# Softmax division with heads on partitions, and a projection of two 128-row products per tile

## The chip, the cores and the metric

One core of one Trainium2 chip runs the kernel. The metric is device time in microseconds from launch to end; lower is better. The engines are TensorE (PE in the rows, its weight loads PEld), VectorE (DVE), ScalarE (ACT), GpSimd (POOL) and SyncE (SP, which issues most transfers). Each runs its own queue in order, and they meet through semaphores.

## What is computed

The input is 16 images of 16x16 positions with 96 channels, that is 4096 tokens. A group norm and a mixture of five 96x96 experts come first, then attention over each image's 256 tokens, then a mixture of four feed-forward experts. The change concerns the attention:

```python
k = jnp.einsum('btc,hcd->bhtd', x, wk)
q = jnp.einsum('btc,hcd->bhtd', x, wq)
v = jnp.einsum('btc,hcd->bhtd', x, wv)
wei = jnp.einsum('bhtd,bhsd->bhts', k, q) / C ** 0.5
wei = jnp.where(causal, wei, -jnp.inf)
wei = jax.nn.softmax(wei, axis=-1)
out = jnp.einsum('bhts,bhsd->bhtd', wei, v)
out = out.transpose(0, 2, 1, 3).reshape(B, T, C)
out = out @ wproj + bproj
```

There are 6 heads of 16 channels. All values are float32.

## The kernel before, in words

The work is cut into 8 units of two images (4 tiles of 128 tokens). Each unit goes through some fifteen kinds of step: `xt` and the group norm, `conv` (first experts), `mix`, `norm1_t`, `qk`, `v`, `score`, `shift`, `prob`, `pv`, `out_t`, `heads_t`, `proj`, `norm2_t`, `gate2`, `ffn1` (12 blocks) and `ffn2` (4 experts). The table `ORDER` lists for each engine, as text, every step in the order in which that engine runs it; `pv.0@3` is part 0 of `pv` of unit 3, and on PE a number behind a colon is the PSUM bank. So the order of work is fixed by hand, on every engine, for all 8 units, and a step that comes late holds up all steps behind it on its engine. `warm` steps (line 800) are matmuls on constants whose results nobody reads; there are 153 of them, nearly all in the first 95 us.

The steps that the change touches, for one unit:

- `pv` (line 931) multiplies the unnormalised probabilities by `v_aug`, which holds 16 channels of V, a column of ones and 15 columns of zeros per head. Its output has heads on partitions: 32 partitions per head (16 channels, the softmax sum in the 17th, zeros), 4 heads side by side, tokens along the row. Twelve head-images make 3 "rounds"; `pv.0` makes two rounds in one bank (128x512), `pv.1` the third (128x256).
- ScalarE copies both banks to `att_t` (line 750).
- `out_t` (line 940): six transposes on PE put tokens on partitions. VectorE then takes the reciprocal of 12 sums per token (line 1182) and multiplies (line 1186) into `att`, once for each of two halves.
- `heads_t` (line 947): four transposes bring `att` back to channels on partitions, in the order of the reference; ScalarE copies it to `heads_t` (line 757), which has a 97th row of ones for the bias.
- `proj` (line 955): one product of 97 rows for each of four tiles. A float32 product is two instructions on PE. VectorE adds the residual (line 1195), takes row statistics, and the second layer norm and the feed-forward part of the unit follow.

On PE the steps of different units are interleaved: while unit n is in attention, PE also runs `ffn1` and `ffn2` of unit n-1 or n-2. One `ffn1` block is three matmuls of 512 columns (lines 787 to 789); one `ffn2` expert is a bias matmul (line 988) and 24 instructions of line 994. VectorE also reduces the scores to row maxima (lines 1152 and 1163), mixes experts (1113 and 1234) and splits values into high and low parts (1131 and 1138).

Of the kernel before, what the change touches and what calls it, by code (L numbers as in the profile page):

```python
# [17 lines left out]
E1 = 4  # L18
# [39 lines left out]
        conv.3@4:6 score.0.0@0:4 score.0.1@0:0 score.0.2@0:3 score.0.3@0:6 score.0.4@0:2 score.1.0@0:5 norm1_t@2:4
        score.1.1@0:0 score.1.2@0:3 score.1.3@0:6 score.1.4@0:4 warm.18@11:2 shift@0:2 qk.0@2:5 qk.1@2:0 warm.2@12:3
        score.0.0@1:3 score.0.1@1:6 score.0.2@1:4 prob.0.0@0:2 score.0.3@1:1 prob.0.1@0:5 score.0.4@1:3 score.1.0@1:6  # L60
        score.1.1@1:4 prob.0.2@0:1 prob.0.3@0:2 prob.0.4@0:3 score.1.2@1:5 prob.1.0@0:1 score.1.3@1:6 prob.1.1@0:4
        score.1.4@1:2 prob.1.2@0:3 prob.1.3@0:5 prob.1.4@0:1 warm.8@13:6 shift@1:6 pv.0@0:4 pv.1@0:2 v@2:3 out_t.0@0:5
        out_t.1@0:1 prob.0.0@1:0 prob.0.1@1:6 prob.0.2@1:4 prob.0.3@1:2 prob.0.4@1:3 heads_t@0:5 prob.1.0@1:0
        prob.1.1@1:1 prob.1.2@1:6 prob.1.3@1:4 proj@0:5 prob.1.4@1:2 warm.3@14:3 score.0.0@2:3 score.0.1@2:0
        score.0.2@2:1 score.0.3@2:6 score.0.4@2:4 score.1.0@2:2 score.1.1@2:5 pv.0@1:3 pv.1@1:0 score.1.2@2:1
        conv.0@5:3 conv.1@5:0 conv.2@5:6 norm2_t@0:4 score.1.3@2:3 score.1.4@2:2 conv.3@5:5 out_t.0@1:0 out_t.1@1:1
        ffn1.0@0:4 ffn1.1@0:3 gate2@0:2 heads_t@1:0 ffn1.2@0:1 ffn1.3@0:6 ffn1.4@0:5 norm1_t@3:0 proj@1:2 shift@2:4
        ffn1.5@0:3 ffn2.0@0:1 ffn2.1@0:6 v@3:4 norm2_t@1:5 ffn1.6@0:2 qk.0@3:3 ffn1.7@0:0 ffn1.8@0:1 ffn1.9@0:4
        ffn1.10@0:2 ffn2.2@0:6 qk.1@3:0 ffn1.11@0:3 prob.0.0@2:1 prob.0.1@2:5 prob.0.2@2:4 prob.0.3@2:2 ffn2.3@0:6
        norm1_t@4:3 prob.0.4@2:0 prob.1.0@2:1 prob.1.1@2:5 prob.1.2@2:4 gate2@1:2 ffn1.0@1:6 prob.1.3@2:0 prob.1.4@2:1  # L70
        conv.0@6:5 conv.1@6:4 conv.2@6:0 conv.3@6:2 ffn1.1@1:1 ffn1.2@1:5 pv.0@2:3 score.0.0@3:4 ffn1.3@1:0 ffn1.4@1:2
        score.0.1@3:6 score.0.2@3:1 ffn1.5@1:3 ffn1.6@1:4 score.0.3@3:5 score.0.4@3:0 pv.1@2:6 score.1.0@3:2
        ffn1.7@1:3 out_t.0@2:1 out_t.1@2:4 score.1.1@3:5 score.1.2@3:6 score.1.3@3:0 score.1.4@3:3 qk.0@4:2 qk.1@4:1
        heads_t@2:4 ffn1.8@1:5 ffn1.9@1:6 ffn1.10@1:4 ffn1.11@1:0 ffn2.0@1:5 proj@2:6 shift@3:3 v@4:4 ffn2.1@1:0
        ffn2.2@1:2 prob.0.0@3:1 conv.0@7:5 norm2_t@2:3 ffn2.3@1:4 prob.0.1@3:6 prob.0.2@3:0 prob.0.3@3:1 prob.0.4@3:5
        norm1_t@5:2 prob.1.0@3:3 prob.1.1@3:6 prob.1.2@3:0 conv.1@7:4 gate2@2:1 prob.1.3@3:5 prob.1.4@3:3
        score.0.0@4:6 ffn1.0@2:0 ffn1.1@2:5 ffn1.2@2:3 ffn1.3@2:1 qk.0@5:4 qk.1@5:2 ffn1.4@2:6 pv.0@3:0 score.0.1@4:5
        score.0.2@4:4 ffn1.5@2:3 score.0.3@4:2 score.0.4@4:1 score.1.0@4:5 conv.2@7:6 conv.3@7:0 score.1.1@4:4
        score.1.2@4:3 score.1.3@4:2 score.1.4@4:6 pv.1@3:1 v@5:0 out_t.0@3:5 out_t.1@3:1 ffn2.0@2:4 shift@4:3
        ffn1.6@2:0 ffn1.7@2:2 ffn1.8@2:6 ffn1.9@2:5 score.0.0@5:1 ffn1.10@2:3 ffn1.11@2:0 heads_t@3:2 score.0.1@5:6  # L80
        prob.0.0@4:4 score.0.2@5:5 prob.0.1@4:3 prob.0.2@4:1 proj@3:0 prob.0.3@4:2 ffn2.1@2:6 ffn2.2@2:5 prob.0.4@4:4
        score.0.3@5:3 score.0.4@5:1 prob.1.0@4:2 prob.1.1@4:0 prob.1.2@4:6 norm2_t@3:4 prob.1.3@4:5 prob.1.4@4:2
        ffn2.3@2:0 gate2@3:6 norm1_t@6:4 score.1.0@5:3 pv.0@4:5 pv.1@4:2 score.1.1@5:1 ffn1.0@3:0 out_t.0@4:6
        out_t.1@4:5 ffn1.1@3:4 qk.0@6:2 score.1.2@5:6 score.1.3@5:5 qk.1@6:0 heads_t@4:4 score.1.4@5:3 v@6:2
        ffn1.2@3:4 ffn1.3@3:0 proj@4:1 ffn2.0@3:2 ffn1.4@3:4 ffn1.5@3:0 ffn1.6@3:6 ffn1.7@3:1 ffn1.8@3:5 ffn2.1@3:4
        shift@5:2 norm2_t@4:0 ffn1.9@3:3 ffn1.10@3:6 ffn1.11@3:1 ffn2.2@3:5 score.0.0@6:2 prob.0.0@5:4 prob.0.1@5:3
        norm1_t@7:0 prob.0.2@5:6 prob.0.3@5:1 ffn2.3@3:5 score.0.1@6:2 prob.0.4@5:4 prob.1.0@5:3 prob.1.1@5:6
# [1177 lines left out]
```

## Time and profile before

| | us |
|---|---|
| median of 3 runs | 353.42 |
| lowest and highest | 352.49, 353.59 |
| the profiled execution's own time | 352.74 |
| its span, first to last instruction | 351.0 |

Busy, in the span: PE 335.9 us, PE's weight loads 273.5, DVE 231.2, ACT 231.8, POOL 107.8. The mean granted clock of TensorE was 0.988 of full speed. Between 100 and 300 us PE was busy for 199.76 of 200 us and VectorE for 139.41. The last chain of work lies for 77% of the span on PE. A mean duration in a group of rows is that of one instruction from start to end; since matmuls overlap, PE's pace is read from the starts of instructions that follow one another or from the chain of waits, not from the mean.

### The profile page before, as it was taken

The page shows a single profiled execution, that of the slowest core. Times are in us where ns is not written, and L with a number is a line of the kernel's source. Part 1 is how long each engine was busy: PE and PEld are TensorE (multiplying, and loading weights), DVE is VectorE, ACT ScalarE, POOL GpSimd, SP SyncE. Part 2 cuts the span into 40 slices and gives each one's busy share as a digit, 9 for nine tenths or more (in the row PEclk, how much of TensorE's full clock was granted, in tenths as well). Part 3 has the DMA queues.
Part 4 walks back from the last instruction along what each step waited for, and adds up shares of the span by engine and source line. Part 5 has one row for each costly group of instructions (what it writes and reads, how often), then busy time and mean ns, then how long its engine had stood idle before and what let it go on. Part 6 is the DMA issues. An engine that isn't in the chain of part 4 may idle for free.

```text
span 351.0 us, 7705 instructions
## 1 busy us (share of the span) xinstructions
PE 335.9 (96%) x2627; PEld 273.5 (78%) x2627; DVE 231.2 (66%) x1025; ACT 231.8 (66%) x467; POOL 107.8 (31%) x179
## 2 busy tenths in 40 slices
PE   6889998879999999999999999999999999999995
PEld 3655466546788987789878988898799789889895
DVE  4859895977379789868686698747647623453232
ACT  3777873555779689548864866497916977374460
POOL 3457761535432224043340434303410305001000
...
GB/s 189 168 4 0 2 35 102 76 63 57 82 3 1 4 67 92 2 52 89 22 69 69 4 23 25 114 5 22 80 57 4 25 2 2 24 1 2 22 2 23
DMA packets 24123, 14.80 MB, mean 42 GB/s; under 512 B 14323, under 2 KB 24083, under 8 KB 24084
## 3 DMA queue, kind: packets, MB, share of 16 engines
...
## 4 chain that ended last, share of the span: by engine, by line
PE 77%; DVE 6%; ACT 6%; DMA 4%; POOL 2%; ACTq 2%; issue 2%; SPq 1%; DVEq 0%; POOLq 0%
PE PS L994 24%; PE PS L787 10%; PE PS L789 9%; PE PS L788 9%; DMA k_stack<-qk_parts 4%; PE PS L931 4%; PE PS L889 3%; PE PS L913 3%; PE PS L840 2%; PE PS L955 2%; PE PS L800 2%; ACTq L684 2%; PE PS L988 2%; PE PS L878 1%; PE PS L940 1%
## 5 line engine op out<-in xcount | busy, mean ns | idle before, releaser
L994 PEld LDWEIGHTS PS<-w_f,hidden 128*128 128x128 f32 x768 | 90.0, 192 | 0.1
L994 PE MATMUL PS<-w_f,hidden 128*128 128x96 f32 x768 | 90.0, 274 | 0.0
L780 ACT ACTIVATE hidden<-PS 128x512 f32<-128x512 f32 x96 | 54.9, 596 | 29.5 <-PE PS L789 27.5
L1234 DVE SCALAR_TENSOR_TENSOR res<-PS,weight,res 128x96 f32<-128x96 f32 x128 | 31.7, 311 | 48.3 <-PE PS L994 48.2
L1152 DVE CUSTOM_DVE_ANT_0 masked<-PS,causal 128x128 bf16<-128x128 f32 (+1 forms) x120 | 35.1, 353 | 9.5 <-PE PS L878 7.4
L787 PE MATMUL PS<-t_hi,w_hi 97*128 97x512 f32 x96 | 40.9, 426 | 0.0
L800 PE MATMUL PS<-ones_b 128*128 128x512 bf16 x153 | 37.0, 391 | 3.4 <-POOL ones_b L518 3.4
L789 PE MATMUL PS<-t_hi,w_lo 97*128 97x512 f32 x96 | 38.1, 397 | 0.0
L788 PE MATMUL PS<-t_lo,w_hi 96*128 96x512 f32 x96 | 38.1, 397 | 0.0
L622 POOL TENSOR_SCALAR_AFFINE_SELECT prob_a<-prob_a 128x768 f32<-128x768 f32 x16 | 13.9, 866 | 65.5 <-ACT prob_a L742 65.5
L1113 DVE SCALAR_TENSOR_TENSOR PS<-conv_y,weight,PS 128x96 f32<-128x96 f32 x128 | 30.3, 315 | 5.1 <-ACT PS L694 5.0
L800 PEld LDWEIGHTS PS<-ones_b 128*128 128x128 bf16 x153 | 14.7, 101 | 20.1 <-issue 5.5
L742 ACT ACTIVATE prob_a<-PS 128x512 f32<-128x512 f32 x48 | 26.1, 610 | 5.9 <-PE PS L913 5.9
L634 ACT ACTIVATE normed<-res,ln_bias,ln_scale 128x96 f32<-128x96 f32 x64 | 24.5, 457 | 2.8 <-POOL ln_bias L543 2.8
L613 POOL TENSOR_SCALAR qk_parts<-qk_rest 96x512 bf16<-96x512 f32 x16 | 9.9, 617 | 49.2 <-DVE qk_rest L1138 32.2
L789 PEld LDWEIGHTS PS<-t_hi,w_lo 97*128 97x128 f32 x96 | 18.2, 190 | 4.3
L533 POOL TENSOR_TENSOR ln_var<-ln_mv,eps_t 128x4 f32<-128x4 f32 x16 | 3.2, 198 | 59.5 <-DVE ln_mv L1045 59.5
L787 PEld LDWEIGHTS PS<-t_hi,w_hi 97*128 97x128 f32 x96 | 18.2, 190 | 3.5 <-issue 0.4
L788 PEld LDWEIGHTS PS<-t_lo,w_hi 96*128 96x128 f32 x96 | 18.2, 189 | 2.7
L679 ACT ACTIVATE conv_y<-PS 128x486 f32<-128x486 f32 x32 | 17.4, 567 | 2.9 <-PE PS L789 2.1
L616 POOL TENSOR_TENSOR qk_parts<-qk_rest,qk_parts 96x512 bf16<-96x512 f32 x16 | 18.5, 1157 | 2.4
L1163 DVE TENSOR_REDUCE row_max<-PS 128x2 f32<-128x512 f32 (+2 forms) x30 | 17.3, 626 | 0.6 <-PE PS L889 0.4
...
## 6 DMA issues: line engine op xcount, KB each, us to landing
...
```

Of the source, the lines that this page charges most:

```text
L616: pool.tensor_tensor(qk_parts[:, tensor, 2, cols], qk_rest[:, tensor, cols], qk_parts[:, tensor, 1, cols], ALU.subtract).then_inc(low_read ...
L634: act.activation(normed[:, which, t, :], rows[:, t, :], ACT.Identity, bias=ln_bias[:, which, t:t + 1], scale=ln_scale[:, which, t:t + 1]). ...
L742: act.activation(dst, PS[:, bank("prob", n, index), 0:dst.shape[1]], ACT.Exp, scale=SCALE).then_inc(act_emptied["prob"], 1)
L780: act.activation(hidden[:, m, 0:T * P], PS[:, bank("ffn1", n, index), 0:T * P], ACT.Gelu).then_inc(act_emptied["ffn1"], 1)
L787: pe.matmul(dst, a_hi, b_hi, start=True, stop=False)
L788: pe.matmul(dst, a_hi[0:b_lo.shape[0], :], b_lo, start=False, stop=False)
L789: return pe.matmul(dst, a_lo, b_hi[0:a_lo.shape[0], :], start=False, stop=True)
L800: pe.matmul(PS[:, bank("warm", n, index), :], ones_b[:, :], ones_b[:, :].unsqueeze(1).to_broadcast([P, 4, P]), start=True, stop=True)
L994: mm = pe.matmul(PS[:, y, t * C:(t + 1) * C], hidden[:, m, t * P:(t + 1) * P], w2_f[:, m, :], start=False, stop=t == T - 1 and c == CHUNKS ...
L1113: ins = dve.scalar_tensor_tensor(mixed[:, t, :], y, weight0[:, t, e:e + 1], mixed[:, t, :], ALU.mult, ALU.add)
L1152: ins = dve.tensor_tensor_reduce(masked[:, place % 2, j * size:(j + 1) * size], ps[:, j * size:(j + 1) * size], causal[:, TOKENS - size:TO ...
L1234: ins = dve.scalar_tensor_tensor(res2[:, t, :], PS[:, y, t * C:(t + 1) * C], weight1[:, t, e:e + 1], res2[:, t, :], ALU.mult, ALU.add).the ...
```

## The change

`out_t` and `heads_t` are gone from every engine, and so are the tiles `inv_sum`, `att` and `heads_t` and ScalarE's two copies of the `pv` banks. In their place VectorE has a step `att` in two parts, for the 512 and the 256 columns that `pv` made. Each part is three instructions on all 128 partitions: `stream_shuffle` reads the `pv` bank and writes, to every partition of a group of 32, the row of that group's 17th partition (the sums); `reciprocal` inverts this whole tile in place; a multiply of the `pv` bank by it writes `att_t`. So `att_t` now holds normalised heads on partitions, with a 1 in each 17th row.

The projection's weight `wproj_r` is stored to match: 128 rows with 16 used of every 32, and 3 slices; row 16 of the first slice holds the bias, all other rows are zero. `proj` is now two accumulated products of 128 rows per tile: one of the image's own four heads, one of the round that holds heads 4 and 5 of both images. `pv` deals the heads to the rounds in that manner. The weight comes in 4 transfers and the bias in one, so that `FFN_LOADS` is 13 instead of 10; the row of ones of `heads_t` needs no transfer any more (`LATE_PADS` 4 instead of 5), and one memset of `wproj_r` (`PADS` 6 instead of 5) is new on VectorE. The tables of all five engines are written anew; there are 154 warm matmuls instead of 153.

```diff
+        wproj_r = sb("wproj_r", [P, 3, C])
-        inv_sum = sb("inv_sum", [P, 2, 2 * HEADS])
-        att = sb("att", [P, TILES, C])
-        heads_t = sb("heads_t", [C + 1, PT])
+        sums = sb("sums", [P, 2 * TOKENS])
...
-        CONV_PADS, PADS, LATE_PADS = 5, 5, 5
-        FFN_LOADS = 10
+        CONV_PADS, PADS, LATE_PADS = 5, 6, 4
+        FFN_LOADS = 13
...
+            wproj_heads = wproj.rearrange("(h d) c -> d h c", d=D)
+            for j in range(HG):
+
+                other = 1 + j // 2
+                ffn_loads.append((wproj_r[HS * j:HS * j + D, 0:other + 1:other, :],
+                                  wproj_heads[:, j:HG + j % 2 + 1:HG + j % 2 - j, :]))
+            ffn_loads.append((wproj_r[D:D + 1, 0, :], bproj.rearrange("(a n) -> a n", a=1)))
...
-                elif kind == "pv":
-                    b = index[0]
-                    wait_filled(act, "pv", n, index)
-                    if n > 0:
-                        wait_filled(act, "out_t", n - 1, (1,))
-                    rounds = (slice(0, 2), slice(2, ROUNDS))[b]
-                    act.activation(att_t[:, rounds, :].rearrange("p r t -> p (r t)"),
...
-                elif kind == "heads_t":
-                    wait_filled(act, "heads_t", n)
...
-                                image, h = divmod(HG * r + j, HEADS)
+                                image, h = ((0, j), (j // 2, HG + j % 2), (1, j))[r]
...
-                elif kind == "out_t":
-                    t = index[0]
-                    wait_bank_free(pe, "out_t", n, index)
-                    wait_act(pe, "pv", n, (1,))
-                    for r in range(ROUNDS):
-                        mm = pe.transpose(PS[:, bank("out_t", n, index), r * P:(r + 1) * P],
-                                          att_t[:, r, t * P:(t + 1) * P], ident[:, :])
-                    mm.then_inc(filled["out_t"], 1)
-                elif kind == "heads_t":
-                    wait_bank_free(pe, "heads_t", n)
-                    wait_dve(pe, "out_t", n, (W - 1,))
-                    for t in range(T):
-                        mm = pe.transpose(PS[0:C, bank("heads_t", n), t * P:(t + 1) * P], att[:, t, :], ident[:, :])
...
-                    wait_act(pe, "heads_t", n)
-                    for t in range(T):
-                        mm = pe.matmul(PS[:, bank("proj", n), t * C:(t + 1) * C], heads_t[:, t * P:(t + 1) * P],
-                                       wproj_f[:, :], start=True, stop=True)
+                    wait_dve(pe, "pv", n, (1,))
+                    for image in range(W):
+                        for half in range(2):
+                            t, rows = 2 * image + half, slice(half * P, (half + 1) * P)
+                            pe.matmul(PS[:, bank("proj", n), t * C:(t + 1) * C], att_t[:, 2 * image, rows], wproj_r[:, 0, :],
+                                      start=True, stop=False)
+                            mm = pe.matmul(PS[:, bank("proj", n), t * C:(t + 1) * C], att_t[:, 1, rows],
+                                           wproj_r[:, 1 + image, :], start=False, stop=True)
...
+            dve.memset(wproj_r[:, :, :], 0.0).then_inc(pad_ready, 1)
...
-                elif kind == "out_t":
...
-                    step_done(dve.reciprocal(inv_sum[:, t, :], rows[:, :, D]))
...
+                elif kind == "att":
+
+                    r = index[0]
+                    rounds = (slice(0, 2), slice(2, ROUNDS))[r]
+                    width = (rounds.stop - rounds.start) * TOKENS
+                    heads = PS[:, bank("pv", n, index), 0:width]
+                    wait_filled(dve, "pv", n, index)
+                    if nth("pv", n, index) > 1:
+                        dve.wait_ge(dve_emptied["pv"], nth("pv", n, index) - 1)
+                    step_done(dve.stream_shuffle(sums[:, 0:width], heads, [D] * HS))
                     wait_step()
+                    step_done(dve.reciprocal(sums[:, 0:width], sums[:, 0:width]))
+                    wait_step()
+                    if n > 0:
+                        wait_filled(dve, "proj", n - 1)
+                    dve.tensor_tensor(att_t[:, rounds, :].rearrange("p r t -> p (r t)"), heads, sums[:, 0:width],
+                                      ALU.mult).then_inc(dve_emptied["pv"], 1)
```

How the instructions stand on the engines is shown at two places. The first is PE in the last unit, unit 7. Before, between the end of `pv` and `proj` stand the last three transposes of `att_t` (line 940), three `ffn1` blocks, the transposes of `att` (line 947), one `ffn2` expert, and then `proj` (line 955):

```order
L940 MATMUL PS<-ident,att_t 128x128 x3
...
L788 MATMUL PS<-t_lo,w_hi 128x512
L789 MATMUL PS<-t_hi,w_lo 128x512
L947 MATMUL PS<-ident,att 96x128 x4
L988 MATMUL PS<-b_parts,ones_b 128x384
L994 MATMUL PS<-w_f,hidden 128x96 x12
L955 MATMUL PS<-wproj_f,heads_t 128x96 x4
```

Now, in the same unit (`pv` is line 918, `ffn1` lines 774 to 776, `ffn2` lines 965 and 971, `proj` lines 930 and 932):

```order
L918 MATMUL PS<-prob_a,v_aug 32x256 x4
L918 MATMUL PS<-prob_b,v_aug 32x128 x4
L774 MATMUL PS<-t_hi,w_hi 128x512
L775 MATMUL PS<-t_lo,w_hi 128x512
L776 MATMUL PS<-t_hi,w_lo 128x512
...
L965 MATMUL PS<-b_parts,ones_b 128x384
L971 MATMUL PS<-w_f,hidden 128x96 x12
L930 MATMUL PS<-wproj_r,att_t 128x96
L932 MATMUL PS<-wproj_r,att_t 128x96
```

No transpose stands there any more; between the last `pv` matmul and the first of `proj` lie two `ffn1` blocks and one `ffn2` expert, and one more `ffn1` block lies between `pv.0` and `pv.1`.

The second place is VectorE in unit 1. Before, the two `out_t` halves stand behind the row maxima of unit 2's scores (line 1163), and the shift of unit 2 follows:

```order
L1163 TENSOR_REDUCE row_max<-PS 128x2 x2
L1182 RECIPROCAL inv_sum<-PS 128x12
L1186 TENSOR_TENSOR att<-PS,inv_sum 128x2x96
L1182 RECIPROCAL inv_sum<-PS 128x12
L1186 TENSOR_TENSOR att<-PS,inv_sum 128x2x96
L1169 TENSOR_SCALAR shift_parts<-row_max 128x4x6
```

Now (row maxima are line 1141):

```order
L1109 TENSOR_TENSOR t2_lo0<-PS,t2_hi0 96x512
L1165 STREAM_SHUFFLE sums<-PS 128x512
L1167 RECIPROCAL sums<-sums 128x512
L1171 TENSOR_TENSOR att_t<-PS,sums 128x512
L1141 TENSOR_REDUCE row_max<-PS 128x2
L1165 STREAM_SHUFFLE sums<-PS 128x256
L1167 RECIPROCAL sums<-sums 128x256
L1171 TENSOR_TENSOR att_t<-PS,sums 128x256
L1141 TENSOR_REDUCE row_max<-PS 128x2
L1147 TENSOR_SCALAR shift_parts<-row_max 128x4x6
```

Two row maxima now stand behind the first and the second part of `att`, and both reciprocals are over all columns.

## Rows read from the trace of the kernel before

**Rows 1.** The page: busy time by engine, and chain that ended last, by engine.
```profile
PE 335.9 (96%) x2627; PEld 273.5 (78%) x2627; DVE 231.2 (66%) x1025; ACT 231.8 (66%) x467; POOL 107.8 (31%) x179
...
PE 77%; DVE 6%; ACT 6%; DMA 4%; POOL 2%; ACTq 2%; issue 2%; SPq 1%; DVEq 0%; POOLq 0%
```

**Rows 2.** Windows of core 0: start:end, length, busy per engine, PEclk, DMA share.
```profile
106.30:146.60 40.30, 40.30 (x320) 34.08 (x320) 34.05 (x158) 33.00 (x68) 11.33 (x17) 1.00 0.14 36
147.20:185.60 38.40, 38.22 (x321) 32.74 (x320) 29.19 (x147) 25.97 (x52) 13.58 (x20) 1.00 0.24 59
...
100.00:300.00 200.00, 199.76 (x1703) 172.82 (x1701) 139.41 (x681) 145.06 (x286) 55.17 (x87) 1.00 0.16 37
```

**Rows 3.** The chain of waits in order of time: start us, us, what.
```profile
143.96 0.45 PE PS L889 x4
...
211.04 0.66 PE PS L940 x6
...
252.47 0.44 PE PS L947 x4
...
259.25 0.89 PE PS L955 x8
```

**Rows 4.** Timeline of PE, units 6 and 7: start us, us, line, out<-in, count.
```profile
297.88 0.64 PE L931 MATMUL PS<-prob_a,v_aug 128*32 128x256 f32 x8
...
299.20 0.61 PE L931 MATMUL PS<-prob_a,v_aug 128*32 128x256 f32 x8
...
308.34 0.39 PE L787 MATMUL PS<-t_hi,w_hi 97*128 97x512 f32 x1
...
309.03 0.39 PE L787 MATMUL PS<-t_hi,w_hi 97*128 97x512 f32 x1
...
310.17 0.33 PE L988 MATMUL PS<-b_parts,ones_b 128*128 128x384 bf16 x1
...
313.18 1.10 PE L955 MATMUL PS<-wproj_f,heads_t 97*128 97x96 f32 x8
```

**Rows 5.** Groups on VectorE by form: count, busy us, mean ns, idle before.
```profile
L1163 DVE TENSOR_REDUCE row_max<-PS 128x2 f32<-128x512 f32 x18 | 11.7, 679 | 0.4 <-PE PS L889 0.4
...
L1138 DVE TENSOR_TENSOR qk_rest<-PS,qk_parts 96x512 f32<-96x512 f32 x16 | 10.5, 680 | 6.5 <-ACT qk_parts L716 6.5
...
L1163 DVE TENSOR_REDUCE row_max<-PS 128x2 f32<-128x256 f32 x6 | 2.5, 412 | 0.0
```

**Rows 6.** The same view: reciprocals, and other small instructions beside them.
```profile
L1182 DVE RECIPROCAL inv_sum<-PS 128x12 f32<-128x12 f32 x16 | 3.6, 226 | 10.4 <-PE PS L940 10.3
...
L1221 DVE RECIPROCAL gpinv<-gpeps 128x4 f32<-128x4 f32 x8 | 1.4, 178 | 0.3
...
L1219 DVE SCALAR_TENSOR_TENSOR gpeps<-gsum,gpsum 128x4 f32<-128x4 f32 x8 | 1.4, 174 | 0.3
L1202 DVE COPY gcross<-PS 128x16 f32<-128x16 f32 x8 | 1.4, 173 | 6.8 <-PE PS L968 6.7
```

**Rows 7.** Timeline of VectorE, the `out_t` pair of unit 3 and its neighbour.
```profile
185.40 0.23 DVE L1182 RECIPROCAL inv_sum<-PS 128x12 f32<-128x12 f32 x1
...
186.47 0.25 DVE L1027 TENSOR_TENSOR beats<-conv_y 128x100 f32<-128x100 f32 x1
```

**Rows 8.** Groups on ScalarE by form: the copies of `pv` and `heads_t`.
```profile
L750 ACT ACTIVATE att_t<-PS 128x512 f32<-128x512 f32 x8 | 4.8, 598 | 6.3 <-PE PS L931 6.3
L757 ACT ACTIVATE heads_t<-PS 96x512 f32<-96x512 f32 x8 | 4.7, 591 | 1.3 <-PE PS L947 1.3
...
L750 ACT ACTIVATE att_t<-PS 128x256 f32<-128x256 f32 x8 | 3.1, 384 | 2.0 <-PE PS L931 1.6
```

**Rows 9.** Timeline of SP's queue in the first 20 us.
```profile
11.96 1.22 SPq L468 DMA_DIRECT2D hidden<-in_L_ffn_b_dram  x3
```

**Rows 10.** Timeline of VectorE: its first instruction after the memsets.
```profile
7.22 0.75 DVE L1052 BATCH_NORM_STATS2 gn_stats<-XT 96x6 f32<-96x256 f32 x2 [3.54 <-ACT XT L641]
```

**Rows 11.** Timeline of ScalarE: its first step that waits for the feed-forward loads.
```profile
21.22 0.19 ACT L655 ACTIVATE gate_both<-gate_f 97x4 fp32r<-97x4 f32 x1
```

More of the change, by code:

```diff
@@ L58 @@
[L58 to L87, printed above, removed]
@@ L98 @@
[L98 to L102 removed]
+        gavg.0@1:2 warm.6@3:4 gavg.1@1 warm.2@4:4 conv.0@0:4 conv.1@0:3 conv.2@0:5 conv.3@0:6 gavg.0@2:0 warm.4@5:1
@@ new lines @@
+        prob.0.0@3:1 ffn2.2@1:5 prob.0.1@3:0 prob.0.2@3:4 prob.0.3@3:3 ffn2.3@1:2 norm2_t@2:6 prob.0.4@3:1
+        prob.1.0@3:5 prob.1.1@3:0 conv.0@7:4 conv.1@7:3 conv.2@7:1 prob.1.2@3:6 prob.1.3@3:5 prob.1.4@3:4
+        score.1.0@4:2 conv.3@7:3 gate2@2:1 ffn1.0@2:0 ffn1.1@2:6 score.1.1@4:2 ffn1.2@2:3 score.1.2@4:5 norm1_t@5:4
+        pv.0@3:1 pv.1@3:2 ffn1.3@2:0 ffn1.4@2:5 ffn1.5@2:6 ffn1.6@2:3 ffn1.7@2:4 ffn1.8@2:0 score.1.3@4:5
+        score.1.4@4:6 ffn1.9@2:3 proj@3:1 qk.0@5:4 shift@4:2 ffn1.10@2:0 ffn1.11@2:5 ffn2.0@2:3 qk.1@5:6 ffn2.1@2:2
@@ new lines @@
+        score.1.2@2 mix.1@4 norm2_t@0 att.0@1 score.1.3@2 att.1@1 score.1.4@2 shift@2 gate2@0 proj@1 norm1_t@3 mix.2@4
+        gates.0@5 weights@0 qk.0@3 mix.3@4 mix.4@4 ffn2.0@0 qk.1@3 xadd@4 gates.1@5 ffn2.1@0 stats1@4 mix.1@5
+        norm2_t@1 ffn2.2@0 mix.2@5 mix.3@5 gate2@1 score.0.0@3 norm1_t@4 score.0.1@3 score.0.2@3 gates.0@6 qk.0@4
+        qk.1@4 att.0@2 score.0.3@3 score.0.4@3 score.1.0@3 ffn2.3@0 score.1.1@3 att.1@2 mix.4@5 weights@1 gates.1@6
+        score.1.2@3 score.1.3@3 score.1.4@3 shift@3 ffn2.0@1 ffn2.1@1 score.0.0@4 score.0.1@4 proj@2 score.0.2@4
@@ new lines @@
+        score.0.3@4 xadd@5 score.0.4@4 stats1@5 ffn2.2@1 mix.1@6 mix.2@6 norm2_t@2 ffn2.3@1 mix.3@6 score.1.0@4
+        mix.4@6 gate2@2 score.1.1@4 score.1.2@4 weights@2 norm1_t@5 att.0@3 att.1@3 score.1.3@4 score.1.4@4 shift@4
+        proj@3 gates.0@7 xadd@6 qk.0@5 ffn2.0@2 stats1@6 qk.1@5 ffn2.1@2 gates.1@7 ffn2.2@2 mix.1@7 mix.2@7 mix.3@7
+        mix.4@7 norm2_t@3 ffn2.3@2 norm1_t@6 gate2@3 qk.0@6 score.0.0@5 score.0.1@5 weights@3 qk.1@6 score.0.2@5
+        score.0.3@5 att.0@4 score.0.4@5 score.1.0@5 score.1.1@5 ffn2.0@3 att.1@4 ffn2.1@3 score.1.2@5 score.1.3@5
```

206 lines of the change are left out of this document (99 added, 107 removed).

## The prediction

> **What bounds the kernel now.** I read the page first [rows 1]: PE is busy for 96% of the span, VectorE and ScalarE for 66% each, and the chain that ended last lies for 77% on PE. A share over the whole span hides stages, so the windows come next [rows 2]: from 100 to 300 us PE is busy for 199.76 of 200 us at full clock. So every PE instruction taken out after 100 us is worth its pace, and every microsecond that PE is made to wait there is lost whole, since nothing behind it can be caught up by a full engine. In the same 200 us VectorE has 60.6 us without work, but not evenly: in the two stretches that lie between the `out_t` steps of units 1, 2 and 3 it is busy for 34.05 of 40.3 and 29.19 of 38.4 us.
>
> **What PE saves.** The pace comes from the chain [rows 3]: six transposes of `att_t` take 0.66 us, four of `att` 0.44, eight instructions of `proj` 0.89, so each is 0.11 us whatever it is. Per unit 10 transposes go (1.10 us) and `proj` grows from 8 to 16 instructions (4 tiles, 2 products, 2 instructions each; +0.89 us). The net is 0.21 us, in 8 units **-1.7 us**. The move from 97 to 128 rows and the new head order in `pv` change no count. The 153 warm matmuls become 154, at 0.22 us nothing.
>
> **What ScalarE saves.** 24 copies, 12.6 us of busy time [rows 8]. ScalarE is not what PE waits for (66% busy, PE idle 0.24 us in 200), so I take nothing for it; it only gives its other steps more room.
>
> **What VectorE pays.** Removed per unit are two pairs of reciprocal and multiply; four instructions take 1.07 us from start to the neighbour's start [rows 7]. Added are two triples. The shuffle and the multiply read a PSUM bank: two instructions of quite different kinds over 512 columns take 0.68 us, one over 256 takes 0.41 [rows 5]; I take these for both. No shuffle is in the trace, so its cost is bounded only by these rows, from 0.6 to, if it ran at half their rate, 1.2 us.
>
> The reciprocal is the term that decides. The trace has it only small [rows 6]: 12 elements take 226 ns, 4 elements 178 ns, while other instructions of 4 or 16 elements take 174 and 173. The line through the two is 6.0 ns per element and 154 ns to start: 53 ns above the plain copy for 12 elements, and 4 for 4. Part of the 53 could belong to the reading from PSUM with a stride, in which case a reciprocal would cost like any instruction. So the bounds for 512 columns are 0.65 us (like the rows of 512 columns, from SBUF slightly less) and 154 + 512 x 6.0 = 3.23 us. The two ends differ five-fold. I take the upper, because the copy from PSUM of 16 elements shows that PSUM alone costs nothing extra at this size, and stays 53 ns below with more elements. For 256 columns it is 1.69 us.
>
> The Trainium skill, "VectorE: DVE Perf Modes", in its walkthrough of the 8-slice pipeline, says that the reciprocal is an iterated hardware divide with a repeat count of 8. Read as 8 cycles of its 0.96 GHz per element, that would be an estimate of 8.3 ns per element and 4.4 us for 512 columns; the rows lie lower, at 6.0 ns. It speaks against this change, since the work goes from 12 sums per token to a copy of each sum on every partition and column.
>
> So one `att.0` is 0.68 + 3.23 + 0.68 and two gaps of 0.06 and one to start, 4.8 us; `att.1` is 0.41 + 1.69 + 0.41 and the same gaps, 2.65 us; a unit's chain is **7.5 us** from the end of `pv.0` to the start of `proj`, where before it was copies, transposes and the pairs. Over 8 units VectorE's busy time rises by about 8 x 6.2 = 50 us, to some 280.
>
> **Where PE waits for it.** For each unit I sum what the new order puts on PE between the end of `pv.0` and `proj`, and what it puts on VectorE. The prices [rows 4]: `pv.1` 0.65 us (`pv.0` 1.3, from start to start), an `ffn1` block 0.69, an `ffn2` expert with its bias matmul 3.0 (310.17 to 313.18); transposes and score matmuls are 0.11 each [rows 3].
> - Units 6 and 7: `pv.1`, three `ffn1` and one `ffn2`: 5.7 us against 7.5, so 1.8 us of wait each.
> - Unit 5: `pv.1`, three `ffn1`, four transposes and four score matmuls, 3.6 us: 3.9 us of wait.
> - Unit 4: `att.0` starts late behind two score steps, and three more and an `ffn2` step stand between its parts; 12.3 us on VectorE against 11.9 on PE: 0.4.
> - Unit 3: six `ffn1`, two scores, one `ffn1` and `pv.1`, 6.0 us: 1.5.
> - Unit 2: over 18 us of PE work: none.
> - Unit 1: `pv.1`, two scores, `gate2` and four `ffn1`, 4.9 us; VectorE has a row maximum of 0.68 between the parts, 8.1: 3.2.
> - Unit 0: `pv.1`, `shift`, `v` and five warm matmuls, 3.4 us, so up to 4.1; but PE is not full there, and the new order has the `qk` splits of unit 2 earlier on VectorE, before the scores of unit 1. I take 1.0.
>
> That is 13.6 us. These are waits of a full PE, in order, one behind the other, so they add.
>
> **What else stands behind it on VectorE.** Behind each `att` part are row maxima, `mix`, `ffn2` sums; PE needs their banks. Between units 1, 2 and 3 VectorE had 6.3 and 9.2 us free in the stretches [rows 2], and part of that is gaps between dependent small instructions which no other step can use. The added 6.4 us (7.5 less 1.07) just fills them. I take 4 us of further waits in units 1 to 4, from a lower bound of 0 to 12 (if each of four units loses half of 6.2).
>
> **The start.** The memset of `wproj_r`, even at the 0.68 us of a 512-column instruction, falls into VectorE's idle 3.54 us [rows 10]. Three more transfers cost SP about 0.4 us each (three of line 468 took 1.22) [rows 9]; the last load is issued at 13.2 us now and by 15 then, and its first reader on ScalarE starts at 21.22 us [rows 11]. Nothing, as long as that cover of some 6 us holds; if it were gone, 1 to 2 us. The order of the first 80 us is also new; its chains are the same, and I give it 0 with 1.5 us to either side.
>
> **The sum** against the profiled execution: 352.74 - 1.7 + 13.6 + 4.0 = 368.6 us. The profiled execution was 0.7 below the median of the runs, so for a median that is **369 us**.
>
> **Rivals.**
> *The reciprocal is as cheap as other instructions.* Then `att.0` is 2.1 us and `att.1` 1.4 with gaps, a chain of 3.5 us, and that fits under the PE work of every unit above (3.4 to 18). VectorE rises by some 19 us and still has room. What is left is PE's 1.7 us: 351 profiled, **351.7** as a median, faster by 0.5%. The point from which it decides is a reciprocal below about 1.5 us for 512 columns. For it speaks that a line through two small sizes is extrapolated forty-fold; against it, that the excess appears in both. 0.12.
> *VectorE becomes the bound.* In the stretch from 100 to 200 us its load and the additions meet PE's length. If half of the added 50 us shows on PE instead of 18, then 352.7 - 1.7 + 25 = 376, and with the steps behind it queued in order up to 384. This is also where a reciprocal of 8.3 ns would lead: by the page's figure, 1.8 us more for a unit's chain, 7 units, so 12.6 on top of 369, that is 382. For it speaks VectorE's 84% in the first stretch; against it, 65% and less after 200 us. **376 to 384**, 0.20.
> *The waits hide each other.* Direct waits fall where PE would have waited for ScalarE's `gelu` or the masks anyway, or the stack transfers come earlier because VectorE's `qk` steps do. Before, PE waited 0.24 us in 200, so there is little to hide in; the new order may have made some. **355 to 361**, 0.10.
> My forecast, 361 to 376, has 0.58.
>
> **How the numbers follow.** A measurement of this kernel can tell about 0.3% (1.1 us) from no change. Faster by more than that is most of the first rival, 0.09; within it 0.03, the rest of that case; slower 0.88. The range from 357 to 384 holds the forecast, the second rival nearly whole and a part of the third; the cheap reciprocal and the tail above are left out. The time of the likeliest case is 369.
>
> **What would show it.** In the profile of the changed kernel the rows of line 1167 must show about 3.2 us for 512 columns and 1.7 for 256; at 0.65 the first rival holds, at 4.4 the page's reading. PE's `proj` row (line 930) should name VectorE's `att_t` (line 1171) as what ended its idle time, with some 14 us in about 7 waits and the longest in units 0, 1 and 5; PE's busy share from 100 to 300 us should fall to about 92%. VectorE's busy time should be near 280 us, ScalarE's near 219. If line 1167 is dear but PE is as full as before, the order covers it and my sums of the PE work are wrong.

## The result, and the profile after

| | before | after |
|---|---|---|
| median of 4 runs, us | 352.96 | 390.28 |
| lowest and highest | 351.76, 353.59 | 389.35, 391.1 |
| profiled span | 351.0 | 388.3 |
| PE busy; PE idle in the span | 335.9; 15.1 | 355.5; 32.8 |
| VectorE busy, ScalarE busy | 231.2, 231.8 | 278.2, 216.2 |
| mean granted clock of TensorE | 0.988 | 0.928 |

The changed kernel takes 1.106 times as long (95% interval 1.104 to 1.109): 37.3 us more, where 16 were forecast, and above the range's end of 384. The sign was right, the size was not. The kernel before has one run more here than in the table ahead of the prediction, which moves its median from 353.42 to 352.96.

The page of the changed kernel, engine by engine, the granted clock in 40 slices (tenths of full speed), the chain by engine, and the groups of the two lines that the prediction named; it answers to [rows 1]:

```profile
PE 355.5 (92%) x2612; PEld 286.0 (74%) x2612; DVE 278.2 (72%) x1058; ACT 216.2 (56%) x441; POOL 107.9 (28%) x179
...
PEclk9999999786987999999968969999699998996999
...
PE 69%; DVE 20%; ACT 4%; issue 3%; POOL 2%; DMA 1%; ACTq 1%; DVEq 0%; POOLq 0%
...
L1167 DVE RECIPROCAL sums<-sums 128x512 f32<-128x512 f32 (+1 forms) x16 | 40.8, 2553 | 0.6
...
L930 PE MATMUL PS<-wproj_r,att_t 128*128 128x96 f32 x64 | 17.5, 367 | 15.9 <-DVE att_t L1171 15.9
```

The clock row of the page of before, which no row ahead of the prediction showed:

```profile
PEclk9999999889999999999999999999999999999999
```

Read the first row against [rows 1] before anything else. The span grew by 37.3 us, and PE's two halves share that: 17.7 us more without work, and 19.6 us more **busy**, though PE has 1.7 us less to do. A busy time that grows with less work means slower instructions. The clock row says why: after the first 80 us it never showed less than a 9 before, and now nine slices have an 8, 7 or 6. The groups of VectorE by form (count, busy us, mean ns, idle before) give the new steps' prices:

```profile
L1167 DVE RECIPROCAL sums<-sums 128x512 f32<-128x512 f32 x8 | 26.8, 3353 | 0.3
L1167 DVE RECIPROCAL sums<-sums 128x256 f32<-128x256 f32 x8 | 14.0, 1753 | 0.3
L1165 DVE STREAM_SHUFFLE sums<-PS 128x512 f32<-128x512 f32 x8 | 5.9, 732 | 0.0
L1171 DVE TENSOR_TENSOR att_t<-PS,sums 128x512 f32<-128x512 f32 x8 | 5.5, 692 | 0.3
```

PE's waits (engine, line, what it waited for: us in all, times, longest):

```profile
PE PS L930 <- DVE att_t L1171: 15.9, 7, 4.5
PE PS L774 <- DVE att_t L1171: 3.8, 3, 1.9
```

Ten waits, 19.7 us: `proj` waits for `att_t`, and so does an `ffn1` block (line 774) at three places where its PSUM bank is the one that `pv` held. The longest is in unit 0, where the timeline of PE (start us, us, line, in brackets the idle time before) shows it, and what comes behind:

```profile
87.01 1.25 PE L787 MATMUL PS<-ones_b 128*128 128x512 bf16 x5
92.74 0.71 PE L930 MATMUL PS<-wproj_r,att_t 128*128 128x96 f32 x2 [4.47 <-DVE att_t L1171]
93.24 0.63 PE L932 MATMUL PS<-wproj_r,att_t 128*128 128x96 f32 x2
93.67 0.64 PE L930 MATMUL PS<-wproj_r,att_t 128*128 128x96 f32 x2
94.09 0.63 PE L932 MATMUL PS<-wproj_r,att_t 128*128 128x96 f32 x2
```

A pair of `proj` instructions now starts every 0.43 us, 0.213 for each instruction, where [rows 3] had 0.11. The windows of the changed kernel (start:end, length, busy of PE, PEld, DVE, ACT, POOL, granted clock, DMA share, GB/s) show the clock there, in the stretch of 100 to 300 us of [rows 2], and behind the waits of units 0, 3 and 5:

```profile
100.00:300.00 200.00, 188.30 (x1475) 159.20 (x1474) 157.25 (x630) 116.83 (x240) 52.38 (x84) 0.92 0.17 36
92.70:96.20 3.50, 3.46 (x16) 3.50 (x17) 0.00 (x0) 0.00 (x0) 0.00 (x0) 0.50 0.02 5
...
197.00:203.80 6.80, 6.78 (x26) 5.55 (x27) 4.83 (x27) 1.11 (x2) 1.34 (x3) 0.50 0.00 1
...
275.00:281.90 6.90, 6.90 (x28) 5.73 (x29) 4.62 (x24) 1.19 (x2) 1.48 (x5) 0.53 0.01 2
281.90:286.00 4.10, 4.10 (x39) 3.90 (x39) 1.60 (x5) 1.44 (x4) 3.52 (x5) 1.00 0.00 0
```

A granted clock of 0.50 is 1.2 GHz in place of 2.4. Read the windows in pairs: from 275.0 to 281.9 PE is busy without a gap and gets 28 instructions done; in the 4.1 us that follow it does 39. The two windows hold different instructions (the first has six of 512 columns), so `proj` gives the fair comparison: a pair every 0.43 us here, and every 0.22 us in unit 4, where the clock stayed at 1.00. The busy share is 100% in both windows, which is why the share of PE's busy time alone tells nothing of this loss.

The mean clock gives the total. Time at half clock is twice the span times what the mean lacks of 1: 2 x 388.3 x 0.072 = 55.9 us after, 2 x 351.0 x 0.012 = 8.4 us before. The most that this can cost is half of the difference, **23.8 us**. PE's busy time shows 19.6 + 1.7 = **21.3 us** of it. The rest is half clock in which PE had nothing to run anyway, inside its waits and behind its last instruction: within the stretches of half clock PE is busy for 49.6 us after and 6.8 before, and half of that difference is 21.4. So the 37.3 us of span are 17.7 of idle time, 21.3 of slow clock, and 1.7 saved.

### The profile page after: what moved, and what is told of

It reads as the page before. It is cut to its first block, busy times and chain, and to the rows that moved or that the text cites. A ratio compares the mean times of both kernels' runs of the same rounds, so it can differ in the third digit from the quotient of the medians.

```text
span 388.3 us, 7660 instructions
## 1 busy us (share of the span) xinstructions
PE 355.5 (92%) x2612; PEld 286.0 (74%) x2612; DVE 278.2 (72%) x1058; ACT 216.2 (56%) x441; POOL 107.9 (28%) x179
## 4 chain that ended last, share of the span: by engine, by line
PE 69%; DVE 20%; ACT 4%; issue 3%; POOL 2%; DMA 1%; ACTq 1%; DVEq 0%; POOLq 0%
PE PS L971 19%; DVE sums L1167 10%; PE PS L774 8%; PE PS L775 7%; PE PS L776 7%; PE PS L787 6%; PE PS L930 3%; PE PS L900 3%; PE PS L932 3%; DVE sums L1165 2%; DVE att_t L1171 2%; PE PS L918 2%; PE PS L827 2%; PE PS L876 1%; PE PS L904 1%
## 5 line engine op out<-in xcount | busy, mean ns | idle before, releaser
L971 PEld LDWEIGHTS PS<-w_f,hidden 128*128 128x128 f32 x768 | 93.0, 197 | 0.0
L971 PE MATMUL PS<-w_f,hidden 128*128 128x96 f32 x768 | 92.4, 278 | 0.0
L774 PE MATMUL PS<-t_hi,w_hi 97*128 97x512 f32 x96 | 43.2, 450 | 3.8 <-DVE att_t L1171 3.8
L1167 DVE RECIPROCAL sums<-sums 128x512 f32<-128x512 f32 (+1 forms) x16 | 40.8, 2553 | 0.6
L775 PE MATMUL PS<-t_lo,w_hi 96*128 96x512 f32 x96 | 39.7, 413 | 0.0
L776 PE MATMUL PS<-t_hi,w_lo 97*128 97x512 f32 x96 | 39.5, 412 | 0.0
L744 ACT ACTIVATE prob_a<-PS 128x512 f32<-128x512 f32 x48 | 26.1, 602 | 15.1 <-PE PS L900 15.0
L930 PE MATMUL PS<-wproj_r,att_t 128*128 128x96 f32 x64 | 17.5, 367 | 15.9 <-DVE att_t L1171 15.9
L787 PEld LDWEIGHTS PS<-ones_b 128*128 128x128 bf16 x154 | 14.7, 101 | 19.6 <-issue 5.8
L930 PEld LDWEIGHTS PS<-wproj_r,att_t 128*128 128x128 f32 x64 | 13.9, 268 | 18.4 <-issue 13.2
L774 PEld LDWEIGHTS PS<-t_hi,w_hi 97*128 97x128 f32 x96 | 19.5, 203 | 9.7 <-DVE att_t L1171 5.1
L718 ACT ACTIVATE qk_parts<-PS 96x512 bf16<-96x512 f32 x16 | 8.9, 592 | 21.8 <-PE PS L776 17.6
```

The source lines that it names most:

```text
L744: act.activation(dst, PS[:, bank("prob", n, index), 0:dst.shape[1]], ACT.Exp, scale=SCALE).then_inc(act_emptied["prob"], 1)
L774: pe.matmul(dst, a_hi, b_hi, start=True, stop=False)
L775: pe.matmul(dst, a_hi[0:b_lo.shape[0], :], b_lo, start=False, stop=False)
L776: return pe.matmul(dst, a_lo, b_hi[0:a_lo.shape[0], :], start=False, stop=True)
L787: pe.matmul(PS[:, bank("warm", n, index), :], ones_b[:, :], ones_b[:, :].unsqueeze(1).to_broadcast([P, 4, P]), start=True, stop=True)
L930: pe.matmul(PS[:, bank("proj", n), t * C:(t + 1) * C], att_t[:, 2 * image, rows], wproj_r[:, 0, :], start=True, stop=False)
```

## Experiments

All are one core and one launch; each ratio is to the kernel before on the same chip. The kernel before took 351.87 us beside e1 to e4, 352.55 beside e5 to e8 and 352.96 beside the changed kernel, so a difference between the medians of two different kernels is good to about 1 us. Two theories stood at the outset. **A**: the long reciprocal makes PE wait some 20 us, and each wait is followed by a stretch of half clock that costs about as much again. **B**: the waits alone are not the cause; VectorE's work as a whole, or the new PE part (`pv` and `proj` in 128 rows), makes the kernel longer.

### Fill the waits with work nobody reads (e1_fill)

84 more warm matmuls stand in front of the instructions that waited, about as long as the waits; nothing else is changed. Two of the nine places:

```diff
-        pv.1@0:4 shift@1:3 v@2:6 warm.5@17:5 proj@0:5 prob.0.0@1:1
+        pv.1@0:4 shift@1:3 v@2:6 warm.25@17:5 proj@0:5 prob.0.0@1:1
...
-        score.1.4@4:6 ffn1.9@2:3 proj@3:1 qk.0@5:4
+        score.1.4@4:6 ffn1.9@2:3 warm.12@20:4 proj@3:1 qk.0@5:4
```

> The changed kernel, with warm matmuls (0.22 us each) added on PE in front of the places where its trace shows PE waiting for att_t: 20 more in unit 0, 6 and 7 in unit 1, 12 in unit 3, 5 in unit 4, 8 and 8 in unit 5, 10 in unit 6, 8 in unit 7. Nothing that is used is computed otherwise. In the trace of the changed kernel PE is without work for 32.8 us (15.1 before) and the granted clock is 0.5 in some 58 us (10 before). Theory A, the waits and the half clock that follows each of them: the waits stay (18 us), the half clock goes, time 370 to 374 us, mean clock above 0.97. Theory B, VectorE's load is the bound and PE's clock only shows that PE has less to do: time stays at 388 to 392 us, the warm matmuls change nothing. Theory C, the clock costs half of what its share suggests: 380.

Measured: 374.3 us (373.65 to 377.45), ratio 1.065 (1.061 to 1.070). The kernel does 18.6 us more on PE than the changed one and is 16.0 us shorter (15 if each is set against the kernel before on its own chip). Its page, its waits for `att_t`, and one new wait:

```profile
PE 358.2 (95%) x2696; PEld 279.4 (74%) x2696; DVE 277.3 (74%) x1058; ACT 215.9 (57%) x441; POOL 107.6 (29%) x179
...
PEclk9999999989978999999999969999999999999999
```

```profile
PE PS L787 <- ACT hidden L767: 2.9, 2, 2.2
...
PE PS L774 <- DVE att_t L1171: 0.5, 1, 0.5
...
PE PS L930 <- DVE att_t L1171: 0.2, 1, 0.2
```

VectorE does the same work in the same order, so what went is not its load. In the profiled execution PE's idle time fell from 32.8 to 17.5 us and the matmuls added 18.6, so by themselves they made the kernel 3.3 us longer; the span is 12.6 us shorter all the same, so the clock gave back 15.9. The time at half clock fell from 55.9 to 2 x 375.7 x 0.023 = 17.3 us, worth up to 19.3. Theory A holds: a little over half of the loss sits in the clock. The profiled run of this kernel was its longest (clock 0.977, against 0.988 to 0.994 in the others), so by medians the clock gives back 18 to 19; the size is good to about 3 us.

Three stretches of half clock are left in this trace before the end. One lies behind a wait for a stack transfer, as in the changed kernel. One begins within the wait of 2.2 us in the first row above, in which the added matmuls themselves wait for a bank. The third, from 218.1 to 224.9 us, has no wait ahead of it; it comes back under "What stays open".

### Leave the reciprocal out (e2_cheap)

```diff
-                    step_done(dve.reciprocal(sums[:, 0:width], sums[:, 0:width]))
+                    step_done(dve.tensor_copy(sums[:, 0:width], sums[:, 0:width]))
```

The division is left out; every wait, tile and table stays.

> The changed kernel with the reciprocal of the sums replaced by a copy of the same tile in place, so the division is left out; all waits and all other instructions stay. A copy of 512 columns should take 0.3 to 0.7 us instead of 3.35, VectorE's busy time falls by 33 us or more. Theory A and B alike say that the reciprocal's length is the whole cause: 351 to 353 us, clock near 0.985, PE's 1.7 us saving just visible. If something else in the new order, the two products or the 13 loads costs time, the result is above 355.

Measured: 350.38 us (349.25 to 351.91), ratio 0.9955 (0.9938 to 0.9972). The group of line 1167, and the page's engines:

```profile
PE 332.4 (96%) x2612; PEld 269.2 (77%) x2612; DVE 244.9 (70%) x1058; ACT 215.7 (62%) x441; POOL 107.8 (31%) x179
```

```profile
L1167 DVE COPY sums<-sums 128x512 f32<-128x512 f32 x8 | 4.1, 507 | 0.3
```

One line sets the whole loss. A unit's two reciprocals are (3.35 - 0.51) + (1.75 - 0.29) = 4.3 us longer than the copies, 34.4 us of VectorE in 8 units, and the kernel is 39.9 us longer for it. It is also the prediction's first rival, played out: with a cheap step in this place the change is 0.45% **faster** than before, 1.5 us, which is about PE's 1.7 us. Theory B's second half falls: the new PE part is as good as was reckoned.

### Take the reciprocal off the chain, but keep its work (e3_off_chain)

The copy stands in the chain as above, and the two reciprocals run behind the multiply into a tile that nobody reads. The division is left out here too.

```diff
-                    step_done(dve.reciprocal(sums[:, 0:width], sums[:, 0:width]))
+                    step_done(dve.tensor_copy(sums[:, 0:width], sums[:, 0:width]))
...
+                    step_done(dve.reciprocal(spare[:, 0:width], sums[:, 0:width]))
+                    wait_step()
```

> As the kernel with the copy in the reciprocal's place (the division is left out), but the same reciprocals (512 and 256 columns per unit) are made behind the multiply of each part, into a tile that nobody reads. VectorE's load is that of the changed kernel plus the copies, about 285 us; only the first part's multiply and its bank come 3 us earlier, while the second part still stands behind the first reciprocal. Theory A, the chain from pv to proj is what PE waits for: the chain falls from 7.5 to about 6 us, the third of it that lay in the second reciprocal is gone, so the waits fall from 18 to 5 to 9 us and the clock loss with them: 360 to 372. Theory B, the load: 386 to 392.

Measured: 383.38 us (381.07 to 384.81), ratio 1.089 (1.085 to 1.093). This is outside what either theory gave, and against me: I had thought that off the chain most of the price would go. PE's waits, and three rows of VectorE's timeline at the place where unit 2's first part is done:

```profile
PE PS L931 <- DVE att_t L1172: 9.6, 7, 3.3
...
PE PS L886 <- DVE shift_parts L1155: 2.5, 3, 1.3
...
PE PS L775 <- DVE row_max L1142: 1.8, 1, 1.8
PE PS L775 <- DVE row_max L1131: 1.6, 1, 1.6
```

```profile
149.36 0.69 DVE L1172 TENSOR_TENSOR att_t<-PS,sums 128x512 f32<-128x512 f32 x1
149.97 3.34 DVE L1174 RECIPROCAL spare<-sums 128x512 f32<-128x512 f32 x1
153.34 0.43 DVE L1131 CUSTOM_DVE_ANT_0 masked<-PS,causal 128x256 bf16<-128x256 f32 x1
```

The masks and row maxima of the next unit stand directly behind the reciprocal in VectorE's queue and start when it ends. Half of the waits for `att_t` are gone, since only the first part's reciprocal still stands ahead of the second part; in their place come waits for `shift_parts` and `row_max`. Their sum, with the 9.6, is 15.5 us. So it is not the dependence alone that costs but the 3.35 us in an in-order queue, wherever PE is this full: theory A's "chain of `att`" was too narrow, and half of B is right, in that whoever is queued behind pays.

### The same reciprocals in the kernel before (e4_before_recip)

The kernel before, with a reciprocal of 512 and one of 256 columns of a spare tile ahead of each unit's two `out_t` parts.

```diff
+                    width = 2 * TOKENS if t == 0 else TOKENS
+                    step_done(dve.reciprocal(spare[:, 0:width], spare[:, 0:width]))
+                    wait_step()
```

> The kernel before with one idle reciprocal of 512 columns ahead of the first out_t half and one of 256 ahead of the second on VectorE, in a tile that nobody reads: the old transposes and the old projection with VectorE's new cost (5.1 us per unit). Summing as in the prediction what its order puts on PE between the transposes and heads_t (1 to 2.6 us in units 0, 1, 2, 4, 5, 8 in unit 3), PE waits some 20 us. Theory A: 352.7 + 20 + about 20 for the half clock, 385 to 400 us, so the changed kernel's new PE part is innocent. Theory B, load: VectorE at 272 of 352 us still has room, 355 to 365. If the new PE part or the new order were at fault: 353 to 358.

Measured: 403.17 us (402.09 to 404.69), ratio 1.146 (1.143 to 1.150), somewhat above what was expected. PE's waits for `att`:

```profile
PE PS L948 <- DVE att L1191: 19.9, 6, 5.2
PE PS L890 <- DVE att L1191: 4.3, 2, 2.4
...
PE PS L788 <- DVE att L1191: 3.1, 2, 2.4
```

The old kernel, whose table was not written for such a step, suffers more: 27.3 us of waits, PE's busy time 356.7 in place of 335.9. This leaves the new tables of the changed kernel as no cause; they soften the blow, if anything.

### Order on PE alone (e6_order)

In units 3 and 6, steps that need nothing from `att` are moved ahead of `proj`; VectorE's list is untouched.

```diff
-        score.1.4@4:6 ffn1.9@2:3 proj@3:1 qk.0@5:4 shift@4:2 ffn1.10@2:0 ffn1.11@2:5 ffn2.0@2:3
+        score.1.4@4:6 ffn1.9@2:3 qk.0@5:4 ffn1.10@2:0 ffn2.0@2:3 proj@3:1 shift@4:2 ffn1.11@2:5
...
-        ffn2.0@5:6 proj@6:0 shift@7:4
-        ffn2.1@5:3 ffn2.2@5:5
+        ffn2.0@5:6 ffn2.1@5:3 proj@6:0 shift@7:4
+        ffn2.2@5:5
```

> The changed kernel with PE's table changed in two units only: in unit 3 qk.0 of unit 5, ffn1.10 and ffn2.0 of unit 2 stand before proj instead of behind it (4.4 us of work against a wait of 2.7), in unit 6 ffn2.1 of unit 5 (2.8 us against 2.2). VectorE's work and order are untouched. Theory A: the two waits (4.9 us) and the half clock behind them (3.4 us each, 5 where the stretch at 0.5 is 10 us long) go: 377 to 382 us against 390. Theory B (VectorE's load): 388 to 392, since VectorE does the same in the same order.

Measured: 381.43 us (381.22 to 383.12), ratio 1.084 (1.081 to 1.086).

```profile
PE 349.3 (92%) x2612; PEld 281.3 (74%) x2612; DVE 276.9 (73%) x1058; ACT 215.9 (57%) x441; POOL 107.5 (28%) x179
```

```profile
PE PS L930 <- DVE att_t L1171: 9.8, 5, 4.5
```

Seven waits of `proj` became five, 6.1 us less in sum, but PE's idle time fell by 2.7 us only, since new waits came (the longest, 1.3 us, for a stack transfer). The span is 8.9 us shorter: 2.7 less idle time, and 6.2 less **busy** time for the same 2612 instructions. Again the clock pays more than the waits themselves.

### One wait, and one wait filled (e7_one_wait, e8_one_filled)

To see the price of a single stretch, the kernel before gets the two spare reciprocals in unit 5 only (e7); in e8, in addition, 18 warm matmuls stand ahead of `heads_t@5`.

```diff
+                    width = 2 * TOKENS if t == 0 else TOKENS
+                    if n == 5:
+                        step_done(dve.reciprocal(spare[:, 0:width], spare[:, 0:width]))
+                        wait_step()
```

```diff
-        heads_t@5:6 ffn1.9@4:4 ffn2.0@4:5
+        warm.18@18:6 heads_t@5:6 ffn1.9@4:4 ffn2.0@4:5
```

> The kernel before with idle reciprocals of 512 and 256 columns on VectorE in unit 5 alone, ahead of the two out_t halves. In the run that had them in all units PE waited 4.1 us there before heads_t. Theory A: one wait of 4.1 us and one stretch of half clock of 6.8 us, worth 3.4 us where PE is full: 351.9 + 7.5, so 358.5 to 360. Theory B: VectorE is half idle in that stretch, so the wait alone at most: 352 to 356.

> As the kernel with reciprocals in unit 5 alone, and 18 warm matmuls (3.9 us) on PE before heads_t of unit 5, in the place of the wait. Theory A: the wait stays as warm work, the half clock goes: 351.9 + 4.1, so 355.5 to 356.5, 3 us or more below the same kernel without them. If the clock has no part in it: the same time as without them.

Measured: e7 358.06 us (357.73 to 359.3), ratio 1.018 (1.015 to 1.020); e8 356.46 (355.17 to 357.97), ratio 1.012 (1.009 to 1.014). e7 lies just below what was expected of it and e8 at the upper end. The timeline of PE in e7 behind the wait, and the same window of 15 us in before, e7 and e8, in this order:

```profile
255.75 1.06 PE L948 MATMUL PS<-ident,att 128*96 128x128 f32 x4 [4.08 <-DVE att L1192]
```

```profile
250.00:265.00 15.00, 15.00 (x124) 13.87 (x122) 8.28 (x50) 6.73 (x14) 1.52 (x4) 1.00 0.35 75
```

```profile
250.00:265.00 15.00, 10.92 (x74) 9.64 (x73) 8.69 (x24) 3.04 (x6) 0.00 (x0) 0.89 0.32 64
```

```profile
250.00:265.00 15.00, 14.91 (x101) 11.44 (x100) 10.25 (x31) 4.85 (x8) 0.93 (x1) 1.00 0.36 80
```

One wait of 4.1 us, and a clock of 0.89 in the window: (1 - 0.89) x 15 x 2 = 3.3 us at half clock, worth 1.7. In e8 the wait's time is still spent, on matmuls that nobody reads, but the clock stays at 1.00, and the kernel is 1.6 us shorter. I had expected 3 us or more, since I took a stretch of 6.8 us as in the changed kernel; here it was 3.3. The mechanism held, the size was half. The 1.6 us rests on the medians of five and six runs, whose mean granted clocks are 0.988 and 0.995 on average (worth up to 2.5 us). The two profiled executions show it only in this window: e7's was its shortest run and e8's its longest, their spans are 356.0 and 356.2 us, and e7 has one stretch of half clock fewer in its first 80 us. What a wait costs beyond itself was thus 1.6 us in this place. Over the changed kernel there were 21.3 us of slow clock beside 19.7 us of waits, though up to 3.4 of the 21.3 lie in a stretch that has no wait ahead of it.

### The division with 16 and 8 elements (e5_turned)

If only the number of elements is at fault, the division should be free with fewer. This kernel computes the whole result: it transposes the `pv` bank in blocks of 32x32, so that the sums of a block's 32 tokens stand in one column, takes the reciprocal of 16 (or 8) such columns, and transposes that column, repeated 32 times, back into the tile of factors.

```diff
-                    step_done(dve.stream_shuffle(sums[:, 0:width], heads, [D] * HS))
+                    blocks = width // HS
+                    step_done(dve.transpose(turned[:, 0:width], heads))
...
-                    step_done(dve.reciprocal(sums[:, 0:width], sums[:, 0:width]))
+                    step_done(dve.reciprocal(inverse[:, 0:blocks],
+                                             turned[:, 0:width].rearrange("p (b d) -> p b d", d=HS)[:, :, D]))
+                    wait_step()
+                    step_done(dve.transpose(sums[:, 0:width].rearrange("p (b d) -> p b d", d=HS),
+                                            inverse[:, 0:blocks].unsqueeze(2).to_broadcast([P, blocks, HS])))
```

> The changed kernel, complete, with the same division made on few elements: VectorE transposes the pv bank in blocks of 32x32, so that the sums of a block stand in one column; the reciprocal is over 16 (8) elements instead of 512 (256); a second block transpose of the inverted column, read 32 times, spreads it over the 32 partitions; then the multiply. Orders are untouched. From the trace of the changed kernel: 0.73 + 0.25 + 0.7 + 0.69 and gaps, 2.6 us for the first part and 1.7 for the second, a chain of 4.3 us against 7.5 there and 3.4 in the kernel with the copy, 0 to 1 us of PE wait in unit 0 and none elsewhere. Theory A: 350 to 354 us, clock above 0.98. If a transpose of blocks runs at half rate or does not take a repeated input at full rate, 355 to 365. Theory B (load): VectorE is at about 255 us, 350 to 354 too; this run is for the version, not for telling A from B.

Measured: 352.32 us (351.78 to 355.01) against 352.55, ratio 1.002 (0.9995 to 1.0046): no difference from before that can be measured, and 38 us shorter than the changed kernel. Five of its twelve runs took 354.7 to 355.0 us at a mean granted clock of 0.979, the other seven 351.8 to 352.6 us at 0.988 to 0.995; no trace shows where the half clock of those five lies. Its groups on VectorE, and PE's wait for it:

```profile
L1173 DVE STREAM_TRANSPOSE sums<-inverse 128x512 f32<-128x512 f32 x8 | 5.7, 711 | 0.3
L1168 DVE STREAM_TRANSPOSE turned<-PS 128x512 f32<-128x512 f32 x8 | 5.7, 710 | 4.4 <-PE PS L920 4.4
...
L1170 DVE RECIPROCAL inverse<-turned 128x16 f32<-128x16 f32 x8 | 2.0, 253 | 0.3
L1170 DVE RECIPROCAL inverse<-turned 128x8 f32<-128x8 f32 x8 | 1.6, 204 | 0.3
```

```profile
PE PS L932 <- DVE att_t L1178: 1.6, 2, 1.0
```

Four instructions take 0.71 + 0.25 + 0.71 + 0.69 = 2.4 us where the changed kernel's three take 4.8. PE's busy time is 333.6, close to e2's 332.4. The span is 2.3 us above e2's, the best that this layout has shown; I found no version that clearly beats the kernel before.

## Why the prediction missed

**PE's own work** (-1.7 us): right. It shows wherever the clock does not hide it: e2 is 1.5 us shorter than the kernel before.

**The prices on VectorE**: right. The reciprocal was forecast at 3.23 and 1.69 us and took 3.35 and 1.75; of the two ends of that bound, five-fold apart, the upper was the true one, and the small excess of [rows 6] was the sign of it. The shuffle took 0.73 against 0.68. A unit's chain ran from 84.92 to 92.6 in unit 0, 7.7 us against 7.5. VectorE's busy time is 278.2 against 280, ScalarE's 216.2 against 219.

The Trainium skill, "VectorE: DVE Perf Modes", in its walkthrough of the 8-slice pipeline, gives the repeat count of 8 that I had read as 8.3 ns per element. It does not fit as I read it: between 256 and 512 columns the trace gives (3353 - 1753) / 256 = 6.25 ns. The measurement decides, and the second rival's 382, which rested on 8.3, has no ground.

**The waits**: right in sum, by luck in part. PE's idle time rose by 17.7 us against 13.6 + 4.0 = 17.6, but the first term was 6 us too small and the second 6 us too large. By unit, the direct waits were:

| unit | 0 | 1 | 2 | 3 | 4 | 5 | 6 | 7 | sum |
|---|---|---|---|---|---|---|---|---|---|
| forecast | 1.0 | 3.2 | 0 | 1.5 | 0.4 | 3.9 | 1.8 | 1.8 | 13.6 |
| measured | 4.5 | 3.1 | 0.5 | 2.7 | 1.1 | 3.8 | 2.2 | 1.9 | 19.7 |

The method (PE's work between two steps against VectorE's chain) gave units 1, 5, 6 and 7 to within 0.4 us. Unit 0 was reckoned at up to 4.1 and then talked down to 1.0 because PE was "not full there"; it measured 4.5, so the reckoned number was the near one. The prediction's own list of signs named unit 0 among the longest waits, against the 1.0 in its sum. Another sign, PE's busy share from 100 to 300 us, came out at 94% where 92 was forecast. The 4.0 us for steps queued behind did not come as extra idle time: beside `att_t` the other waits shrank by 2.0. That second term was not empty of sense, though: e3 shows those steps paying, as soon as `att` itself no longer does.

**The step that failed** is the sum itself: "352.74 - 1.7 + 13.6 + 4.0". It lets a wait cost its own length and lets the work behind it run at the pace of [rows 3]. Nowhere did I price the clock. It is the whole miss: 21.3 of the 21.4 us between the profiled execution's own 390.0 and 368.6. The sign of it was on the page of before: its clock row has an 8 in the two slices from 61 to 79 us, where PE had waited 1.1 and 1.8 us for transfers of `k_stack`. I read that row only for the stretch from 100 to 300 us.

By the rule of the Trainium skill, "TensorE: Matmul & The Clock Gate", in its part on oscillation of the clock gate, the penalty is the time throttled times (1 - 1.2/2.4), that is half of it; the trace agrees, with 21.3 us of added busy time under the 23.8 that this gives, and 21.4 when the half clock is counted only where PE was busy.

**The rivals.** VectorE as the bound would have given 376 to 384; the time lies above even that, but not by this mechanism: VectorE is busy for 72% of the span and, in the stretch from 100 to 200 us that this rival named, for 86.6 of 100 us, and e1 takes 16 us off without touching it. The cheap reciprocal at 351.7 is what e2 measured at 350.4. The waits hid little of one another: beside those for `att_t` the others shrank by 2.0 us, where the third rival needed 8 or more. The range, 357 to 384, was put together from the same terms as the sum, so it could not hold what none of them held.

**What stays open.** Of the stretches of half clock in the changed kernel seven lie behind a wait or begin within one: they run from 73.3 to 80.1 (a wait of 2.5 us for a stack transfer), 90.3 to 97.2 (unit 0), 114.2 to 121.1 (unit 1), 196.1 to 206.4 (unit 3), 274.7 to 281.5 (unit 5), 319 to 322.4 (unit 6) and 349.8 to 356.6 (unit 7). The program's last microsecond is another. One, from 223.5 to 230.3, has no wait ahead of it: PE has been busy without a gap since 197.1, of late with short instructions of `v` and `gate2`. It is no echo of the wait of unit 3: behind the same steps e1 has such a stretch from 218.1 to 224.9, with PE busy for 28.04 of the 28.1 us before it, and e3 one from 225.2 to 232.0. The same PE table in e2 and in e5 shows none at that place. It is worth up to 3.4 of the 21.3 us, and what draws it no experiment isolates. And not every wait has its stretch. These rows of PE's timeline in the changed kernel, of units 4 and 6, show no fall, and one that begins 1.5 us late:

```profile
245.19 0.43 PE L930 MATMUL PS<-wproj_r,att_t 128*128 128x96 f32 x2 [1.13 <-DVE att_t L1171]
```

```profile
317.76 0.43 PE L930 MATMUL PS<-wproj_r,att_t 128*128 128x96 f32 x2 [2.21 <-DVE att_t L1171]
...
319.26 0.64 PE L930 MATMUL PS<-wproj_r,att_t 128*128 128x96 f32 x2
```

Which wait draws a stretch of 3.4, 6.8 or 10.2 us, and which none, these runs do not settle.
